# Product-key experts: a tile's output added to x in the eighth head, the differences to the best sum formed by GpSimd

## The chip, the cores and the metric

The kernel runs on one core of a Trainium2 chip. The metric is the device time of one execution in microseconds (us). The core has a matrix engine (TensorE, PE in the profile; its weight loads are PEld), a vector engine (VectorE, DVE), an activation engine (ScalarE, ACT), a general engine (GpSimd, POOL) and SyncE (SP), which only starts transfers here. Each engine works through its own queue in order; they meet at semaphores. SBUF is the on-chip memory of 128 partitions, PSUM the memory that TensorE writes.

## What is computed

The program is a stack of twelve layers on x of 128 x 32 tokens with 128 features, so 4096 rows. The change lies in the third one, a feed-forward layer with product keys. Cut to what matters, for each row of the normalised x:

```
# 8 heads, 2 x 32 keys per head, 1024 experts (i, j), the best 8 are kept
sx = query_x @ keys_x            # 32 similarities per head
sy = query_y @ keys_y            # 32 similarities per head
s[i, j] = sx[i] + sy[j]          # 1024 sums per head
best = the 8 largest s           # among pairs of the 8 best sx and the 8 best sy
share = softmax(best)            # over these 8
value[e] = gelu_tanh(x . down[e])
out = sum over heads and kept experts of share * value[e] * up[e]
x = x + out
```

The kernel does it without gathering: in place of the eight experts it works over all 1024, with exp(s - best) set to zero below the eighth best sum, and divides by the sum of the eight exponentials.

## The kernel before

The 4096 rows are 32 tiles of 128 rows (one per partition). `product_key_experts` first folds the query weights and keys (`query_keys`) and then runs one block in which each engine has a function `phase(t, s, before, after)` for tile t; `s` is the buffer of two, `before` is true where a tile comes ahead of t, `after` where one or two follow. `over_tiles` calls the phases in the same order on all engines, so the work around the change is ordered by hand, by the line at which a step stands in `phase`.

A phase has eight heads, h = 0 to 7, called the first to the eighth head here. Per head:

- GpSimd forms the 1024 sums of two similarities (L751) into one of four buffers, when the product four heads back has freed it. It waits for nothing else but, in the first head, the similarities.
- ScalarE takes the exponential of each half of 512 into a PSUM bank, with minus the best sum as its bias (L790), and scales the identity by the reciprocal of the total into `share` (L795).
- VectorE masks and copies each half: `prob` = (sum >= eighth best) * exponential (L866), the "masking product".
- TensorE multiplies `prob` by `share` in eight blocks (L933, two instructions each) and adds up over the heads in PSUM.

Between the heads stand the steps for the neighbouring tiles. On VectorE, in order: `weigh` of tile t - 1 in the first head (L855, its end lets TensorE start the output, L918, in the fourth head); moments of x of tile t + 2 in the third (L119, L122); bias and MAX8 over the similarities of tile t + 1 in the fourth and fifth (L820, L826); in the sixth the addition of tile t - 1's output to x (L878 to L880, helper L173), which waits for TensorE's `out_done`, and then the cube of the gelu (L846); in the seventh `bests` of tile t + 1 (L829): eight MAX8 over 64 pair sums (L831), a drain, the subtraction `shift` = best eight - best (L833), the negated best as bias (L835). Behind the eighth head come `invert_totals` (L840, L842), which waits for ScalarE's exponential of `shift`, and `gelu` (L850).

GpSimd has, beside the sums, the normalisation factors of tile t + 2 behind the seventh head (L135, L142, L733) and the pair sums of tile t + 1 behind the eighth (L740), for which it waits until the MAX8 of L826 are done. ScalarE has `shift_exp` of tile t + 1 (L771) behind the eighth head, then a normalisation (L766). The first tile's steps are done in a preamble.

Of the kernel before, what the change touches and what calls it, by code (L numbers as in the profile page):

```python
# [16 lines left out]
ALU = mybir.AluOpType  # L17
# [7 lines left out]
P = 128  # L25
# [145 lines left out]
def add_to_x(core, t, update):  # L171

    return core.nc.vector.tensor_tensor(core.x[:, ds(t, 1), :], core.x[:, ds(t, 1), :], update, ALU.add)  # L173
# [488 lines left out]
def product_key_experts(core, name):  # L662
# [8 lines left out]
    nc, dram = core.nc, core.dram  # L671
    H, K, TOP, KG = 8, 32, 8, 16
    E = K * K
    with ExitStack() as outer:
# [14 lines left out]
        pairs = sb("pairs", [P, H, TOP * TOP])  # L689
        best = sb("best", [P, S, H, TOP])  # L690
        shift = sb("shift", [P, H, TOP])
# [17 lines left out]
        half = lambda t, k: t[:, k * HALF:(k + 1) * HALF]  # L709
        shifted_mean = sb("shifted_mean", [P, S])  # L710
        front = Front(core, outer, f"{name}2", S, lambda s: core.psum[:, 7, 0:P])
        (centred, simmed, sims_ready, topped, paired, valued, squared, cubed, tanhed, gelued, cut, exped, inverted, shared, biased, summed, probs, used, kept,
         mixed, out_done) = (core.sem(f"{name}_{n}") for n in (
             "centred", "simmed", "sims_ready", "topped", "paired", "valued", "squared", "cubed", "tanhed", "gelued", "cut", "exped", "inverted", "shared", "biased", "summed", "probs", "used",
             "kept", "mixed", "out_done"))
        block = outer.enter_context(nc.Block())

        def over_tiles(eng, phase):

            phase(0, 0, False, 2)  # L720
            with eng.Fori(0, TILES // 2 - 2) as it:
                phase(1 + 2 * it, 1, True, 2)
                phase(2 + 2 * it, 0, True, 2)
            phase(TILES - 3, 1, True, 2)
            phase(TILES - 2, 0, True, 1)
            phase(TILES - 1, 1, True, 0)

        @block.gpsimd
        def _(pool):
            def normal_factors(t, s):  # L730
                front.pool_rstd(pool, t - s, only=s)
                pool.drain()
                nc.gpsimd.tensor_scalar(shifted_mean[:, s:s + 1], front.mv[:, s, 0:1], front.rstd[:, s, :], -1.0, ALU.mult,  # L733
                                        ALU.mult).then_inc(centred, 1)

            def pair_sums(t, s):
                pool.wait_ge(topped, t + 1)
                sx = top[:, s, 0:H, :].rearrange("p h (i j) -> p h i j", j=1).to_broadcast([P, H, TOP, TOP])
                sy = top[:, s, H:2 * H, :].rearrange("p h (i j) -> p h i j", i=1).to_broadcast([P, H, TOP, TOP])
                nc.gpsimd.tensor_tensor(pairs[:, :, :].rearrange("p h (i j) -> p h i j", j=TOP), sx, sy,  # L740
                                        ALU.add).then_inc(paired, 1)

            def phase(t, s, before, after):
                for h in range(H):
                    if h == 0:
                        pool.wait_ge(sims_ready, t + 1)

                    pool.wait_ge(kept, (t * H + h + 1) * HALVES)
                    sx = sims[:, s, h, :].rearrange("p (i j) -> p i j", j=1).to_broadcast([P, K, K])
                    sy = sims[:, s, H + h, :].rearrange("p (i j) -> p i j", i=1).to_broadcast([P, K, K])  # L750
                    nc.gpsimd.tensor_tensor(sums[:, h % RING, :, :], sx, sy, ALU.add).then_inc(summed, 1)  # L751
                    if after == 2 and h == 6:
                        normal_factors(t + 2, s)
                if after:
                    pair_sums(t + 1, 1 - s)

            normal_factors(0, 0)
            normal_factors(1, 1)
            pair_sums(0, 0)
            over_tiles(pool, phase)  # L760

        @block.scalar
# [53 lines left out]
        @block.vector  # L816
        def _(dve):
            def add_bias(t, s):
                dve.wait_ge(simmed, t + 1)
                nc.vector.tensor_tensor(sims[:, s, :, :].rearrange("p g k -> p (g k)"), SIMS, b_sim[:, :],  # L820
                                        ALU.add).then_inc(sims_ready, 1)
                dve.drain()

            def tops(s, groups):
                for g in groups:
                    ins = nc.vector.max(top[:, s, g, :], sims[:, s, g, :])  # L826
                return ins

            def bests(t, s):  # L829
                for h in range(H):  # L830
                    nc.vector.max(best[:, s, h, :], pairs[:, h, :])  # L831
                dve.drain()
                nc.vector.tensor_tensor(shift[:, :, :], best[:, s, :, :],  # L833
                                        best[:, s, :, 0:1].to_broadcast([P, H, TOP]), ALU.subtract).then_inc(cut, 1)
                nc.vector.tensor_scalar(bias[:, s, :], best[:, s, :, 0:1].rearrange("p h a -> p (h a)"), -1.0, None,  # L835
                                        ALU.mult).then_inc(biased, 1)

            def invert_totals(t, s):
                dve.wait_ge(exped, t + 1)
                nc.vector.tensor_reduce(total[:, s, :], shift[:, :, :], X, ALU.add)  # L840
                dve.drain()
                nc.vector.reciprocal(total[:, s, :], total[:, s, :]).then_inc(inverted, 1)  # L842

            def cube(t, s):
                dve.wait_ge(squared, t + 1)
                nc.vector.scalar_tensor_tensor(cubic[:, :], cubic[:, :], 1.0, pair(2 * s), ALU.add, ALU.mult).then_inc(cubed, 1)  # L846

            def gelu(t, s):
                dve.wait_ge(tanhed, t + 1)
                nc.vector.scalar_tensor_tensor(value[:, s, :], cubic[:, :], 1.0, pair(2 * s), ALU.add,  # L850
                                               ALU.mult).then_inc(gelued, 1)

            def weigh(t, s):
                dve.wait_ge(used, (t + 1) * H + RING)
                nc.vector.scalar_tensor_tensor(weight[:, :], value[:, s, :], 0.5, pair(2 * s), ALU.mult,  # L855
                                               ALU.mult).then_inc(mixed, 1)

            def phase(t, s, before, after):
                o = 1 - s
                for h in range(H):  # L860
                    dve.wait_ge(used, t * H + h + 1)
                    if after and h == 6:
                        dve.wait_ge(paired, t + 2)
                    for k in range(HALVES):
                        dve.wait_ge(probs, (t * H + h) * HALVES + k + 1)
                        nc.vector.scalar_tensor_tensor(  # L866
                            half(prob[:, h % RING, :], k), half(sums[:, h % RING, :, :].rearrange("p i j -> p (i j)"), k),
                            best[:, s, h, TOP - 1:TOP], raw_prob(k), ALU.is_ge, ALU.mult).then_inc(kept, 1)
                    if before and h == 0:
                        weigh(t - 1, o)  # L870
                    if after == 2 and h == 2:
                        front.dve_moments(dve, t + 2 - s, only=s)
                    if after and h == 3:
                        add_bias(t + 1, o)
                        tops(o, range(0, KG // 2))
                    if after and h == 4:
                        tops(o, range(KG // 2, KG)).then_inc(topped, 1)
                    if before and h == 5:  # L878
                        dve.wait_ge(out_done, t)
                        add_to_x(core, t - 1, OUT)  # L880
                    if after and h == 5:
                        cube(t + 1, o)
                    if after and h == 6:
                        bests(t + 1, o)
                if after:
                    invert_totals(t + 1, o)
                    gelu(t + 1, o)

            front.dve_moments(dve, 0, only=0)
            front.dve_moments(dve, 0, only=1)  # L890
            add_bias(0, 0)
            tops(0, range(KG)).then_inc(topped, 1)
            dve.wait_ge(paired, 1)
            cube(0, 0)
            bests(0, 0)
            invert_totals(0, 0)
            gelu(0, 0)
            over_tiles(dve, phase)
            weigh(TILES - 1, 1)
            dve.wait_ge(out_done, TILES)  # L900
            add_to_x(core, TILES - 1, OUT)
# [2437 lines left out]
```

## Time and profile before

| | us |
|---|---|
| median of 3 runs (lowest to highest) | 3903.31 (3892.4 to 3909.63) |
| the profiled execution | 3910.36 |
| its span, first to last instruction | 3908.2 |
| TensorE busy in the span | 3360.9 (86%) |
| VectorE busy | 2672.6 (68%) |
| ScalarE busy | 1648.2 (42%) |
| GpSimd busy | 1231.1 (31%) |

The stage of the change takes some 690 us of the span, from about 389 to 1084 us. The rows of the trace are read like this: a row of a timeline has the start from the span's start, the duration, engine, line, operation, what it writes <- what it reads with the shape, how many instructions the row merges (xN), and in brackets the idle time of the engine just before it and what ended that. Instructions of one engine overlap a little in the records, so the start of the next is a better measure of an instruction's cost than its own duration.

### The profile page before, as it was taken

Reading aid. Unit: us, or ns where it says so; the run is one execution under the profiler, and the core shown is the slowest. Engines: PE = TensorE matmul, PEld = TensorE weight load, DVE = VectorE, ACT = ScalarE, POOL = GpSimd, SP = SyncE. Lnnn points to the kernel's source line nnn. Section 1 sums busy time; section 2 is a strip of 40 time slices with the busy share of each in tenths; the row PEclk is TensorE's granted clock in tenths of the full one; section 3 lists DMA queues with packets and bytes.
Section 4 is the critical chain, followed back from the end, with each engine's and each line's share of the span. In section 5 each row is a group of like instructions: output and inputs, shape, how many; then the busy total and the mean of one; then the engine's idle time right before and its main releaser. Section 6 shows DMA issues by size and latency. Waiting matters only on the chain. (4 is left out here: it accounts for less than half of the span.)

```text
span 3908.2 us, 106170 instructions
## 1 busy us (share of the span) xinstructions
PE 3360.9 (86%) x39854; PEld 2856.4 (73%) x39856; DVE 2672.6 (68%) x7741; ACT 1648.2 (42%) x4070; POOL 1231.1 (31%) x1704
## 2 busy tenths in 40 slices
PE   3787899999968888797899999999999999874756
PEld 2675788888846666545689999999999999743345
DVE  7774899999948888667355555555555555469776
ACT  1231677777727777564122222222222222223342
POOL 3552788888713333303100000000000000145042
PEclk8897999999979999898699999999999999968677
DMA  3000000000012222200275565556555565355000
GB/s 92 4 0 36 1 0 0 0 0 0 1 42 77 76 75 75 58 1 7 45 134 125 121 125 115 125 124 126 125 114 125 125 127 124 64 100 78 1 3 24
DMA packets 374617, 253.41 MB, mean 65 GB/s; under 512 B 118452, under 2 KB 371336, under 8 KB 373672
## 3 DMA queue, kind: packets, MB, share of 16 engines
q1 hardware_dynamic: 369960, 244.92, 28.9%
q10 hardware_dynamic: 4352, 4.20, 0.5%
q8 instruction: 220, 3.60, 0.4%
q14 instruction: 85, 0.70, 0.1%
HBM read 233.01 MB, written 15.75 MB: 64 GB/s over the span
## 5 line engine op out<-in xcount | busy, mean ns | idle before, releaser
L2146 ACT ACTIVATE L_xattn_prob<-psum,L_xattn_nmax 128x258 f32<-128x258 f32 x512 | 239.2, 472 | 958.4 <-DVE L_xattn_nmax L2178 958.4
L933 PE MATMUL psum<-L_ffn_share,L_ffn_prob 128*128 128x128 f32 x4096 | 495.0, 278 | 54.7 <-DVE L_ffn_prob L866 54.7
L2267 PE MATMUL psum<-L_xattn_ctxT,L_xattn_q_ctx 128*128 128x257 f32 x2048 | 523.2, 388 | 9.0 <-issue 4.7
L933 PEld LDWEIGHTS psum<-L_ffn_share,L_ffn_prob 128*128 128x128 f32 x4096 | 472.1, 193 | 73.8 <-DVE L_ffn_prob L866 58.8
L751 POOL TENSOR_TENSOR L_ffn_sums<-L_ffn_sims 128x1024 f32<-128x1024 f32 x256 | 486.6, 1913 | 106.7 <-DVE L_ffn_prob L866 106.7
L2289 PEld LDWEIGHTS psum<-L_xattn_probT,L_xattn_ctx 32*128 32x128 f32 x16384 | 471.1, 187 | 47.0 <-DVE L_xattn_q_ctx L2169 41.0
L2289 PE MATMUL psum<-L_xattn_probT,L_xattn_ctx 32*128 32x128 f32 x16384 | 496.0, 274 | 4.0 <-DVE L_xattn_probT L2192 2.1
L2122 POOL TENSOR_TENSOR L_xattn_z_var<-L_xattn_z_mv,L_xattn_z_eps 128x1 f32<-128x1 f32 x32 | 6.1, 191 | 1328.8 <-DVE L_xattn_z_mv L2204 1295.8
L2267 PEld LDWEIGHTS psum<-L_xattn_ctxT,L_xattn_q_ctx 128*128 128x128 f32 x2048 | 362.0, 191 | 58.0 <-DMA L_xattn_ctx<-ctx_dram 4.8
L790 ACT ACTIVATE psum<-L_ffn_sums,L_ffn_bias 128x512 f32<-128x512 f32 x512 | 340.4, 688 | 94.1 <-DVE L_ffn_prob L866 89.9
L866 DVE SCALAR_TENSOR_TENSOR L_ffn_prob<-L_ffn_sums,L_ffn_best,psum 128x512 f32<-128x512 f32 x512 | 357.8, 740 | 5.7 <-ACT psum L790 2.4
L1223 ACT ACTIVATE L_xattn_prob<-psum,L_xattn_nmax 128x289 f32<-128x289 f32 x512 | 250.0, 501 | 125.0 <-DVE L_xattn_nmax L1250 125.0
L2253 PEld LDWEIGHTS psum<-L_xattn_xnT,L_xattn_m_h 128*128 128x128 f32 x2048 | 269.8, 194 | 20.0 <-issue 4.6
L2253 PE MATMUL psum<-L_xattn_xnT,L_xattn_m_h 128*128 128x128 f32 x2048 | 274.5, 278 | 3.4 <-DVE L_xattn_q_ctx L2169 2.1
L2169 DVE COPY L_xattn_q_ctx<-psum 128x256 f32<-128x256 f32 x512 | 192.5, 415 | 97.5 <-PE psum L2253 97.2
L2278 PEld LDWEIGHTS psum<-L_xattn_u_h,L_xattn_mixed_ctx 128*128 128x128 f32 x2048 | 233.6, 192 | 3.0 <-ACT L_xattn_mixed_ctx L2157 1.3
L2278 PE MATMUL psum<-L_xattn_u_h,L_xattn_mixed_ctx 128*128 128x128 f32 x2048 | 233.9, 275 | 1.1 <-ACT L_xattn_mixed_ctx L2157 1.1
L1250 DVE TENSOR_REDUCE L_xattn_nmax<-psum 128x1 f32<-128x289 f32 x512 | 198.9, 451 | 46.0 <-PE psum L1290 46.0
L2192 DVE STREAM_TRANSPOSE L_xattn_probT<-L_xattn_prob 128x512 f32<-128x512 f32 x256 | 182.1, 711 | 20.1 <-issue 0.9
L2178 DVE TENSOR_REDUCE L_xattn_nmax<-psum 128x2 f32<-128x516 f32 x256 | 178.0, 695 | 20.2 <-issue 1.7
L2186 DVE TENSOR_SCALAR L_xattn_prob<-L_xattn_prob,L_xattn_total 128x256 f32<-128x256 f32 x512 | 161.8, 358 | 20.3 <-issue 0.4
L1290 PE MATMUL psum<-L_xattn_k_all,L_xattn_q_bd 32*128 32x289 f32 x1024 | 100.2, 461 | 79.3 <-POOL L_xattn_k_all L1187 71.8
(439 smaller groups left out, 6149.5 us busy)
## 6 DMA issues: line engine op xcount, KB each, us to landing
L_xattn_ctx<-ctx_dram SPq DMA_DIRECT2D x512, 256.0 KB, 5.4
L_xattn_ctxT<-ctx_T_dram SPq DMA_DIRECT2D x128, 257.0 KB, 3.1
L_xattn_k_all<-ctx_T_dram SPq DMA_DIRECT2D x128, 128.5 KB, 2.1
L_xattn_v_all<-ctx_dram SPq DMA_DIRECT2D x128, 128.0 KB, 2.3
L_attn_qkv_scratch<-L_attn_qkv SPq DMA_DIRECT2D x24, 256.0 KB, 2.8
L_attn_rows<-L_attn_qkv_scratch SPq DMA_DIRECT2D x24, 256.0 KB, 5.2
start_raw<-ctx_dram ACTq DMA_DIRECT2D x16, 256.0 KB, 12.3
start_plug_all<-plug_scratch SPq DMA_DIRECT2D x1, 2048.0 KB, 7.1
```

The lines of the kernel that those rows point to most:

```text
L751: nc.gpsimd.tensor_tensor(sums[:, h % RING, :, :], sx, sy, ALU.add).then_inc(summed, 1)
L790: nc.scalar.activation(raw_prob(k), half(sums[:, h % RING, :, :].rearrange("p i j -> p (i j)"), k), ACT.Exp, bias=bias[:, s, h:h + 1]).the ...
L866: nc.vector.scalar_tensor_tensor(half(prob[:, h % RING, :], k), half(sums[:, h % RING, :, :].rearrange("p i j -> p (i j)"), k), best[:, s, ...
L933: last = nc.tensor.matmul(pair(2 * s)[:, c * P:(c + 1) * P], prob[:, h % RING, c * P:(c + 1) * P], share[:, h % RING, :], start=(h == 0 an ...
L1223: ins = nc.scalar.activation(prob[:, b % 2, g, :], scores(g), ACT.Exp, bias=nmax[:, b % 2, g:g + 1], accum_out=total[:, b % 2, g:g + 1])
L1250: nc.vector.tensor_reduce(nmax[:, b % 2, g:g + 1], scores(g), X, ALU.max, negate=True).then_inc(maxed, 1)
L2146: ins = nc.scalar.activation(prob[:, s, g, :], scores(s)[:, g, :], ACT.Exp, bias=nmax[:, s, g:g + 1], accum_out=total[:, s, g:g + 1])
L2169: nc.vector.tensor_copy(q_ctx[:, p, c, :, 2 * j:2 * j + 2, :], q_bank(k).rearrange("p (h b n) -> p b h n", h=2, b=BT)).then_inc(q_out, 1)
L2253: last = nc.tensor.matmul(q_bank(k)[:, i * P:(i + 1) * P], m_h[:, 2 * j + i, c * P:(c + 1) * P], tokens(t), start=True, stop=True)
L2267: last = nc.tensor.matmul(scores(s)[:, g, 0:CTX], q_ctx[:, p, c, b, h:h + 4, :].rearrange("p h n -> p (h n)"), ctxT[:, b, c, :], start=(c ...
L2278: nc.tensor.matmul(OUT, mixed_ctx[:, r, c * G + i, :], u_h[:, c, 4 * i + r, :], start=(r + c + i == 0), stop=False)
L2289: last = nc.tensor.matmul(mix_bank(r)[:, c * P:(c + 1) * P], ctx[rows, b, k, c * P:(c + 1) * P], probT[rows, b % 2, k, :, :].rearrange("p ...
```

## The change

The addition of tile t - 1's output to x moves in VectorE's phase from the sixth head to the eighth, behind that head's masking product and ahead of `invert_totals`. The subtraction moves from VectorE to GpSimd: VectorE's last MAX8 increments a new semaphore `bested`, GpSimd's new `differences(t, s)` waits for it and increments `cut`, for which ScalarE waits as before. It stands behind the sums of the third head of tile t, and for the first tile in the preamble, behind the first pair sums. The bias stays on VectorE behind the drain.

```diff
--- before.py
+++ after.py
@@ -709,9 +709,9 @@
         half = lambda t, k: t[:, k * HALF:(k + 1) * HALF]
         shifted_mean = sb("shifted_mean", [P, S])
         front = Front(core, outer, f"{name}2", S, lambda s: core.psum[:, 7, 0:P])
-        (centred, simmed, sims_ready, topped, paired, valued, squared, cubed, tanhed, gelued, cut, exped, inverted, shared, biased, summed, probs, used, kept,
+        (centred, simmed, sims_ready, topped, paired, valued, squared, cubed, tanhed, gelued, bested, cut, exped, inverted, shared, biased, summed, probs, used, kept,
          mixed, out_done) = (core.sem(f"{name}_{n}") for n in (
-             "centred", "simmed", "sims_ready", "topped", "paired", "valued", "squared", "cubed", "tanhed", "gelued", "cut", "exped", "inverted", "shared", "biased", "summed", "probs", "used",
+             "centred", "simmed", "sims_ready", "topped", "paired", "valued", "squared", "cubed", "tanhed", "gelued", "bested", "cut", "exped", "inverted", "shared", "biased", "summed", "probs", "used",
              "kept", "mixed", "out_done"))
         block = outer.enter_context(nc.Block())
 
@@ -740,6 +740,11 @@
                 nc.gpsimd.tensor_tensor(pairs[:, :, :].rearrange("p h (i j) -> p h i j", j=TOP), sx, sy,
                                         ALU.add).then_inc(paired, 1)
 
+            def differences(t, s):
+                pool.wait_ge(bested, t + 1)
+                nc.gpsimd.tensor_tensor(shift[:, :, :], best[:, s, :, :], best[:, s, :, 0:1].to_broadcast([P, H, TOP]),
+                                        ALU.subtract).then_inc(cut, 1)
+
             def phase(t, s, before, after):
                 for h in range(H):
                     if h == 0:
@@ -749,6 +754,8 @@
                     sx = sims[:, s, h, :].rearrange("p (i j) -> p i j", j=1).to_broadcast([P, K, K])
                     sy = sims[:, s, H + h, :].rearrange("p (i j) -> p i j", i=1).to_broadcast([P, K, K])
                     nc.gpsimd.tensor_tensor(sums[:, h % RING, :, :], sx, sy, ALU.add).then_inc(summed, 1)
+                    if h == 2 and before:
+                        differences(t, s)
                     if after == 2 and h == 6:
                         normal_factors(t + 2, s)
                 if after:
@@ -757,6 +764,7 @@
             normal_factors(0, 0)
             normal_factors(1, 1)
             pair_sums(0, 0)
+            differences(0, 0)
             over_tiles(pool, phase)
 
         @block.scalar
@@ -828,10 +836,9 @@
 
             def bests(t, s):
                 for h in range(H):
-                    nc.vector.max(best[:, s, h, :], pairs[:, h, :])
-                dve.drain()
-                nc.vector.tensor_tensor(shift[:, :, :], best[:, s, :, :],
-                                        best[:, s, :, 0:1].to_broadcast([P, H, TOP]), ALU.subtract).then_inc(cut, 1)
+                    last = nc.vector.max(best[:, s, h, :], pairs[:, h, :])
+                last.then_inc(bested, 1)
+                dve.drain()
                 nc.vector.tensor_scalar(bias[:, s, :], best[:, s, :, 0:1].rearrange("p h a -> p (h a)"), -1.0, None,
                                         ALU.mult).then_inc(biased, 1)
 
@@ -875,7 +882,7 @@
                         tops(o, range(0, KG // 2))
                     if after and h == 4:
                         tops(o, range(KG // 2, KG)).then_inc(topped, 1)
-                    if before and h == 5:
+                    if before and h == 7:
                         dve.wait_ge(out_done, t)
                         add_to_x(core, t - 1, OUT)
                     if after and h == 5:
```

## Rows read from the trace of the kernel before

**Rows 1.** Busy time by windows: engines with instructions, granted clock, DMA.

```profile
440.00:1060.00 620.00, 576.76 (x4781) 545.08 (x4781) 565.30 (x1491) 462.87 (x848) 502.32 (x348) 1.00 0.00 0
```

**Rows 2.** Groups by line and form, 440 to 1080 us: busy, mean ns | idle before.

```profile
L833 DVE TENSOR_TENSOR L_ffn_shift<-L_ffn_best 128x64 f32<-128x64 f32 x30 | 29.2, 974 | 2.2
...
L173 DVE TENSOR_TENSOR x_sb<-x_sb,psum 128x128 f32 x28 | 8.1, 288 | 32.4 <-PE psum L918 32.4
...
L135 POOL TENSOR_TENSOR L_ffn_front_var_sb<-L_ffn_front_mv_sb,eps 128x1 f32<-128x1 f32 x28 | 5.4, 193 | 0.0
```

**Rows 3.** Timeline of VectorE, from one sixth head to the next.

```profile
714.21 1.39 DVE L866 SCALAR_TENSOR_TENSOR L_ffn_prob<-L_ffn_sums,L_ffn_best,psum 128x512 f32<-128x512 f32 x2
716.76 0.29 DVE L173 TENSOR_TENSOR x_sb<-x_sb,psum 128x128 f32 x1 [1.16 <-PE psum L918]
716.97 1.21 DVE L846 SCALAR_TENSOR_TENSOR L_ffn_cubic<-L_ffn_cubic,psum 128x1024 f32<-128x1024 f32 x1
718.10 1.40 DVE L866 SCALAR_TENSOR_TENSOR L_ffn_prob<-L_ffn_sums,L_ffn_best,psum 128x512 f32<-128x512 f32 x2
719.41 1.10 DVE L831 MAX8 L_ffn_best<-L_ffn_pairs 128x8 f32<-128x64 f32 x8
720.59 0.98 DVE L833 TENSOR_TENSOR L_ffn_shift<-L_ffn_best 128x64 f32<-128x64 f32 x1
721.49 0.16 DVE L835 TENSOR_SCALAR L_ffn_bias<-L_ffn_best 128x8 f32<-128x8 f32 x1
721.56 1.39 DVE L866 SCALAR_TENSOR_TENSOR L_ffn_prob<-L_ffn_sums,L_ffn_best,psum 128x512 f32<-128x512 f32 x2
722.88 0.21 DVE L840 TENSOR_REDUCE L_ffn_total<-L_ffn_shift 128x8 f32<-128x64 f32 x1
...
730.03 0.29 DVE L119 BATCH_NORM_STATS2 L_ffn_front_stats_sb<-x_sb 128x6 f32 x1 [0.21 <-issue]
...
735.44 1.39 DVE L866 SCALAR_TENSOR_TENSOR L_ffn_prob<-L_ffn_sums,L_ffn_best,psum 128x512 f32<-128x512 f32 x2
```

**Rows 4.** Timeline of GpSimd, the same tile.

```profile
714.38 1.07 POOL L740 TENSOR_TENSOR L_ffn_pairs<-L_ffn_top 128x512 f32<-128x512 f32 x1 [0.27 <-DVE L_ffn_top L826]
715.41 3.78 POOL L751 TENSOR_TENSOR L_ffn_sums<-L_ffn_sims 128x1024 f32<-128x1024 f32 x2
719.58 1.91 POOL L751 TENSOR_TENSOR L_ffn_sums<-L_ffn_sims 128x1024 f32<-128x1024 f32 x1 [0.38 <-DVE L_ffn_prob L866]
723.04 1.91 POOL L751 TENSOR_TENSOR L_ffn_sums<-L_ffn_sims 128x1024 f32<-128x1024 f32 x1 [1.55 <-DVE L_ffn_prob L866]
```

**Rows 5.** Timeline of ScalarE, the same tile.

```profile
721.60 0.26 ACT L771 ACTIVATE L_ffn_shift<-L_ffn_shift 128x64 f32<-128x64 f32 x1 [0.81 <-DVE L_ffn_shift L833]
721.77 0.49 ACT L766 ACTIVATE L_ffn_front_xn_sb<-x_sb,L_ffn_shifted_mean,L_ffn_front_rstd_sb 128x128 f32 x1
722.37 1.32 ACT L790 ACTIVATE psum<-L_ffn_sums,L_ffn_bias 128x512 f32<-128x512 f32 x2
```

**Rows 6.** Timelines of VectorE and GpSimd, preamble and the stage's first tile.

```profile
402.67 1.89 DVE L835 TENSOR_SCALAR L_ffn_bias<-L_ffn_best 128x8 f32<-128x8 f32 x1
...
417.99 1.39 DVE L866 SCALAR_TENSOR_TENSOR L_ffn_prob<-L_ffn_sums,L_ffn_best,psum 128x512 f32<-128x512 f32 x2
...
422.93 2.00 DVE L833 TENSOR_TENSOR L_ffn_shift<-L_ffn_best 128x64 f32<-128x64 f32 x1
...
424.92 1.40 DVE L866 SCALAR_TENSOR_TENSOR L_ffn_prob<-L_ffn_sums,L_ffn_best,psum 128x512 f32<-128x512 f32 x2
...
402.62 3.77 POOL L751 TENSOR_TENSOR L_ffn_sums<-L_ffn_sims 128x1024 f32<-128x1024 f32 x2
...
419.19 5.65 POOL L751 TENSOR_TENSOR L_ffn_sums<-L_ffn_sims 128x1024 f32<-128x1024 f32 x3
```

**Rows 7.** Timeline of TensorE: the output of the tile ahead.

```profile
714.66 1.95 PE L918 MATMUL psum<-L_ffn_up,L_ffn_weight 128*128 128x128 f32 x16
```

## Prediction

> **What bounds the kernel now.** I read the profile from the outside in. The diff touches one stage, the product-key experts, so the first view is the table by windows for the even part of that stage [rows 1]: in 620 us TensorE is busy for 576.76 us (93%), VectorE for 565.30 us (91%), GpSimd for 502.32 us (81%) and ScalarE for 462.87 us (75%), at a granted clock of 1.00. Two engines are nearly full, so the next question is which of them the other waits for. The timeline of VectorE answers it [rows 3]: its instructions follow each other at once, and the one idle time of more than 0.25 us in a tile is the 1.16 us before the addition to x (L173). The groups by line [rows 2] say the same of the sum: 32.4 us of idle time in front of 28 of these additions, 1.16 us each. So VectorE sets the pace with two blemishes: it waits for TensorE's output at L173, and its subtraction L833, 64 elements wide, takes 0.974 us on average [rows 2].
>
> I take as zero of a tile the start of the sixth head's masking product (L866, h = 5): 714.21 in one tile, 735.44 in the next [rows 3]. The period is 21.23 us. Counted from that zero, before: the addition to x at +2.55, the cube L846 at +2.76, the seventh head's product at +3.89, the eight MAX8 at +5.20, the subtraction at +6.38, the bias (L835) at +7.28, the eighth head's product at +7.35 and the sum of the exponentials (L840) at +8.67. Everything from there to the next zero is 21.23 - 8.67 = 12.56 us of VectorE work which the diff leaves alone. So the question is by how much +8.67 moves.
>
> **Why the subtraction is slow.** At +6.38 it starts, and it ends at 721.57. GpSimd's pair sums of the third head (L751) run from 719.58 to 721.49 [rows 4]. In the stage's first tile it starts at 422.93 and ends at 424.93; GpSimd's three sums from 419.19 end at 424.84 [rows 6]. Twice it ends 0.08 to 0.09 us behind GpSimd's instruction, whatever its own length. It is not the subtraction alone: the bias instruction L835, 8 elements, takes 0.16 us in most tiles and 1.89 us at 402.67, where GpSimd had begun a sum at 402.62 that lasts about 1.9 us [rows 6]. Both wait until GpSimd's instruction lets go. This is what the page SBUF — State Buffer of the Trainium skill (section "SBUF: two separate sides") states as an exclusive lock on a shared pair of ports, for VectorE instructions with two SBUF inputs or in a two-port mode; the trace agrees for both kinds (0.98 and 1.89 us). The rule speaks against this change, since the bias, with one input and its output in SBUF, stays on VectorE; a sum that leaves the lock out would be the 2.14 us a tile worked out next.
>
> **Part 1: the addition moves from the sixth head to the eighth.** At its old place it costs the wait and itself: the product at 714.21 is followed at 716.76, and the cube at 716.97. In the first tile, which has no addition there, the same steps run freely [rows 6]: zero at 417.99, the instruction behind the MAX8s at 422.93, which is +4.94 against +6.38. So 1.44 us go. TensorE's output ended at 716.61 [rows 7], +2.40, so at its new place (+8.2) the result has long been there; the wait is free. The addition itself still costs 716.97 - 716.76 = 0.21 us. Its address is computed by a register instruction; the idle "issue" time before L119, which has one too, is 0.21 us [rows 3], so this is between 0 and 0.21 us more. I take 0.03, as there is no drain in front of the addition behind which it would have to stand. Nobody waits for x soon: its moments were taken long before, and the next output of TensorE follows three heads later.
>
> **Part 2: the subtraction leaves VectorE.** Its start to the bias's start was 0.90 us. Taken at face value, both parts give 1.44 + 0.90 - 0.21 = 2.13 to 2.14 us a tile, 64 us over 30 tiles. That is not what I expect. The bias now comes straight behind the MAX8s, at +4.94. GpSimd, counted from the same zero: pair sums at +0.17 (714.38), head 1 at +1.20 (715.41), head 2 at +1.20 + 3.78 - 1.91 = +3.07, and so head 3 at +4.94, unless VectorE holds it up; before it started only at 719.58, +5.37, since it waited for the seventh head's product [rows 4]. With that product 1.44 us earlier, that wait is gone and head 3 starts at +4.94, the very time of the bias. Exactly this is seen in the first tile: GpSimd at 419.19 + 5.65 - 1.91 = 422.93, VectorE at 422.93, and VectorE lost: 2.00 us [rows 6]. There the eighth head's product starts at 424.92; with the bias as the waiting instruction and nothing behind it, at about 424.85, +6.86. Before it was +7.35. So parts 1 and 2 together bring that product forward by 0.49 us, and the addition behind it takes 0.21 to 0.24 back: 0.25 us a tile.
>
> **Part 3: GpSimd's differences.** The trace shows no 64-element instruction on GpSimd. The nearest rows are 0.19 us for one element [rows 2] and 1.07 us for 512 [rows 4]; with 1.91 us for 1024 the slope is 1.64 ns per element and 64 elements come to 0.34 us. I take 0.34, between 0.19 and 1.07. They stand behind head 3's sums, which end at +6.85; done at +7.2. ScalarE's exponential (0.26 us, begun 0.03 us behind the subtraction's end [rows 5]) then ends at +7.5. VectorE needs it at 6.86 + 1.32 + 0.24 = +8.4. It is covered by 0.9 us; were the cover gone, each further us would be a us. On GpSimd the differences have head 4's sums behind them, which wait for the eighth head's product and start at 723.04 after an idle time of 1.5 us [rows 4]; so they cost it nothing. On ScalarE the exponential has a normalisation and the next tile's first exponentials behind it (721.77 and 722.37 [rows 5]), which VectorE wants only 2 us later. The new semaphore costs an increment on the last MAX8, which is nothing here.
>
> **Part 4: the ends.** In the preamble GpSimd now waits for the first tile's MAX8s, until about 402.2, before it sums head 1, where it had finished two sums. VectorE's first bias in turn no longer stands 1.89 us behind GpSimd [rows 6]. I put these at plus or minus 1 us together, once. The last tile ends on TensorE and gains nothing.
>
> **The sum.** 30 tiles have both the addition and the MAX8s. 30 x 0.25 = 7.5 us of the profiled execution's 3910.36 us: 3902.9. The median of the runs shown, 3903.31, is 0.18% below that execution, so in its terms 3903.3 - 7.5 = 3895.8, about 3896. With the register instruction at 0 to 0.21 us and 1 us for the preamble, this case reaches from 3893 to 3903.
>
> **The rivals.** (a) *The bias gets in first.* VectorE and GpSimd arrive within 0.01 us of each other, and whichever is a few hundredths of a us early keeps the other out. If it is the bias, it takes 0.16 us, head 3's sums run from +5.10 to +7.0, the differences end at +7.35, the exponential at +7.64, and L840 starts at +7.67 in place of +8.67; the addition disappears in that wait. That is 1.0 us a tile, 30 us, 3873; so the 2.14 us are out of reach even then, and TensorE, 93% busy, would be close at 19.7 us of 20.2. For it speaks that the tie is so near; against it, that VectorE lost the one tie and the one arrival 0.05 us late that the trace has. A mixture of tiles lies in between; it passes 0.5% when about half to two thirds of the tiles go this way. (b) *The lock goes from GpSimd to GpSimd.* The differences are queued directly behind head 3's sums; if they are served before the bias, it waits 0.34 us longer, the product starts at +7.20, and 0.15 - 0.24 = -0.09 us a tile: 3 us slower, 3906. Against it: at 402.6 VectorE was let in between two sums. (c) *Slower: the differences are slow on GpSimd.* Their broadcast restarts every eight elements, and the trace has no such width. L840 then waits at +6.85 + c + 0.3. From c = 1.2 us the gain shrinks, from 1.52 us it is a loss, and 0.5% is lost from 2.2 us on; at c = 2.5 us it is 1.0 us a tile, 30 us, 3933. Against it: twice the 1.07 us of an instruction with eight times the elements.
>
> **How the numbers follow.** Forecast 0.60, (a) 0.22, (b) 0.12, (c) 0.06. The predicted time is the forecast's, 3896. The range takes in (a) and (b) and leaves (c) out: 3871 to 3909. A measurement here tells 0.5% from no change, 19.5 us. Faster by more than that is (a), 0.22; within it are the forecast and (b), 0.72; slower is (c), 0.06.
>
> **What would show it.** In the changed kernel's trace: no idle time before L173's new place, and none before the cube; the bias instruction at about 1.9 to 2.0 us in nearly every tile, ending 0.08 us behind GpSimd's third sum; GpSimd's third sum directly behind its second; the differences at 0.3 to 0.4 us and no wait of L840 for ScalarE; a period of 20.98 us. A bias of 0.16 us in most tiles with a wait before L840 is (a); one of 2.3 us is (b); a long wait before L840 with long differences is (c). A period under 20 us would say that my account of the two engines' exclusion is wrong.

## The result, and the profile after

Over twenty runs each the changed kernel takes 3881.33 us (median; 3872.95 to 3894.76) and the kernel before 3900.55 us (3892.4 to 3909.63). The ratio is 0.9954 with a 95% interval of 0.9944 to 0.9964: 18 us, 0.46%, faster, with an interval of 14 to 22 us (the medians themselves lie 19.2 us apart). I forecast 7.5 us, and a range of 3871 to 3909 us. The sign and the class (less than 0.5%) came out; the size is more than twice mine. About 5.5 us of that lie in the stage of the change and are explained below; the rest lies outside it.

First where the time lies. The moments of x (L119) mark the stage: their first start here and their first start in the next layer. Columns: how many, shortest/median/longest in ns, first and last start. Before:

```profile
L119 DVE BATCH_NORM_STATS2 L_ffn_front_stats_sb<-x_sb x32: 293/294/296, 389.1 to 1026.5; 128x6 f32 x28, 128x6 f32<-128x128 f32 x4
L119 DVE BATCH_NORM_STATS2 L_xattn_front_stats_sb<-x_sb x32: 274/276/295, 1086.2 to 1133.5; 128x6 f32 x32
```

After:

```profile
L119 DVE BATCH_NORM_STATS2 L_ffn_front_stats_sb<-x_sb x32: 293/294/296, 383.0 to 1008.2; 128x6 f32 x28, 128x6 f32<-128x128 f32 x4
L119 DVE BATCH_NORM_STATS2 L_xattn_front_stats_sb<-x_sb x32: 274/278/295, 1067.1 to 1114.0; 128x6 f32 x32
```

1086.2 - 389.1 = 697.1 us became 1067.1 - 383.0 = 684.1 us: 13.0 us less in the stage (12.9 before rounding). The spans, 3908.2 and 3881.3 us, differ by 26.9 us: 6.1 us of that are there already when the stage begins, and 7.8 us come behind it, and at neither place was an instruction altered. A difference of two single executions is not a measurement of this change; the stage by itself is.

Now the tile. VectorE after, from the start of the sixth head's product (my zero) to the next; L873 is the masking product that was L866, L842 the bias that was L835, L847 the sum that was L840:

```profile
702.20 1.39 DVE L873 SCALAR_TENSOR_TENSOR L_ffn_prob<-L_ffn_sums,L_ffn_best,psum 128x512 f32<-128x512 f32 x2
703.50 1.22 DVE L853 SCALAR_TENSOR_TENSOR L_ffn_cubic<-L_ffn_cubic,psum 128x1024 f32<-128x1024 f32 x1
704.63 1.40 DVE L873 SCALAR_TENSOR_TENSOR L_ffn_prob<-L_ffn_sums,L_ffn_best,psum 128x512 f32<-128x512 f32 x2
705.95 1.11 DVE L839 MAX8 L_ffn_best<-L_ffn_pairs 128x8 f32<-128x64 f32 x8
707.15 1.92 DVE L842 TENSOR_SCALAR L_ffn_bias<-L_ffn_best 128x8 f32<-128x8 f32 x1
708.99 1.39 DVE L873 SCALAR_TENSOR_TENSOR L_ffn_prob<-L_ffn_sums,L_ffn_best,psum 128x512 f32<-128x512 f32 x2
710.31 0.27 DVE L173 TENSOR_TENSOR x_sb<-x_sb,psum 128x128 f32 x1
710.50 0.20 DVE L847 TENSOR_REDUCE L_ffn_total<-L_ffn_shift 128x8 f32<-128x64 f32 x1
...
722.96 1.39 DVE L873 SCALAR_TENSOR_TENSOR L_ffn_prob<-L_ffn_sums,L_ffn_best,psum 128x512 f32<-128x512 f32 x2
```

GpSimd beside it:

```profile
702.37 1.07 POOL L740 TENSOR_TENSOR L_ffn_pairs<-L_ffn_top 128x512 f32<-128x512 f32 x1 [0.27 <-DVE L_ffn_top L834]
703.39 5.65 POOL L756 TENSOR_TENSOR L_ffn_sums<-L_ffn_sims 128x1024 f32<-128x1024 f32 x3
709.00 0.29 POOL L745 TENSOR_TENSOR L_ffn_shift<-L_ffn_best 128x64 f32<-128x64 f32 x1
710.46 1.91 POOL L756 TENSOR_TENSOR L_ffn_sums<-L_ffn_sims 128x1024 f32<-128x1024 f32 x1 [1.17 <-DVE L_ffn_prob L873]
```

Against [rows 3] the wait in front of the cube is gone and so is the subtraction, but the bias, an instruction over eight elements, has grown from 0.16 to 1.92 us. It starts at +4.95 and ends at 709.07 (707.15 + 1.92). GpSimd's three sums no longer pause before the third, as they did in [rows 4]; the third starts at 703.39 + 5.65 - 1.91 = 707.13, 0.02 us ahead of the bias, and ends at 709.04. The eighth head's product comes at +6.79 in place of +7.35, and the addition takes part of that back. The period shown is 20.76 us in place of 21.23 us. Over all 32 tiles the bias has these durations (shortest/median/longest), so it is so nearly everywhere:

```profile
L842 DVE TENSOR_SCALAR L_ffn_bias<-L_ffn_best x32: 300/1920/1928, 396.1 to 1039.0; 128x8 f32<-128x8 f32 x32
```

### The profile page after: what moved, and what is told of

It is laid out like the page before. It is cut to its first block and busy times, and to the rows that moved or that the text cites. A ratio compares the mean times of both kernels' runs of the same rounds, so it can differ in the third digit from the quotient of the medians.

```text
span 3881.3 us, 106172 instructions
## 1 busy us (share of the span) xinstructions
PE 3347.8 (86%) x39856; PEld 2848.1 (73%) x39856; DVE 2692.2 (69%) x7709; ACT 1645.6 (42%) x4070; POOL 1237.4 (32%) x1736
## 5 line engine op out<-in xcount | busy, mean ns | idle before, releaser
L873 DVE SCALAR_TENSOR_TENSOR L_ffn_prob<-L_ffn_sums,L_ffn_best,psum 128x512 f32<-128x512 f32 x512 | 357.7, 739 | 7.9 <-ACT psum L798 3.6
## 6 DMA issues: line engine op xcount, KB each, us to landing
start_raw<-ctx_dram ACTq DMA_DIRECT2D x16, 256.0 KB, 12.2
```

Of the source, the lines that this page charges most:

```text
L873: nc.vector.scalar_tensor_tensor(half(prob[:, h % RING, :], k), half(sums[:, h % RING, :, :].rearrange("p i j -> p (i j)"), k), best[:, s, ...
```

## The experiments

Seven kernels, with 4 to 12 runs each, beside 20 runs of the kernel before for the first four and 9 for the last three. The table has the difference of the medians to the kernel before in the same comparison (before: 3896.66 us beside the first four, 3896.99 us beside the last three), the stage's length in the run's own profile less the 697.1 us of before, and the start of the eighth head's product from my zero. The last column is what is left of the span outside the stage.

| kernel | median us | to before | ratio (95%) | stage, to before | eighth head at | rest |
|---|---|---|---|---|---|---|
| before (profile above) | | | | 697.1 | +7.35 | 3211 |
| after (profile above) | | | | -13.0 | +6.79 | 3197 |
| after_again | 3881.95 | -14.7 | 0.9957 (0.9940 to 0.9973) | -12.8 | | 3201 |
| e1_add_only | 3891.32 | -5.3 | 0.9983 (0.9972 to 0.9993) | -7.4 | +6.92 | 3197 |
| e2_diff_only | 3886.39 | -10.3 | 0.9973 (0.9962 to 0.9984) | -4.8 | +7.22 | 3195 |
| e3_bias_reduce | 3855.00 | -41.7 | 0.9894 (0.9879 to 0.9910) | -39.1 | +5.17 | 3189 |
| e6_split | 3864.18 | -32.8 | 0.9917 (0.9904 to 0.9931) | -34.5 | +5.93 | 3196 |
| e4_diff_first | 3836.50 | -60.5 | 0.9841 (0.9827 to 0.9854) | -60.2 | +5.17 | 3203 |
| e5_both | 3834.55 | -62.4 | 0.9838 (0.9824 to 0.9852) | -60.0 | | 3195 |

### Is the rest of the program part of it?

> The changed kernel unaltered, to separate the stage from the rest. The stage of product-key experts, from its first moments of x to the next layer's, took 697.1 us in the profile before and 684.2 us in the profile after, 12.9 us less, while the medians differ by 19 us. Theory one: the other 6 us are scatter of the rest of the program between executions; then this run's rest (span less the stage) differs from 3197.1 us (that of the profile after) by several us while its stage is again 684 us, and its time lies 13 to 19 us under before. Theory two: the change alters something outside the stage; then the rest is again 3197 us and the time again 19 us under.

The stage is again 12.8 us shorter, from 390.2 to 1074.5 us, while the rest is 3201 us and not 3197 us. Over all nine profiles the rest runs from 3189 to 3211 us, and the profile before is its upper end. In the other six kernels the differences of medians lie from 5.5 us beyond the stage's (e2) to 2.1 us short of it (e1), on both sides. The kernel before itself had a median of 3900.55 us in the first comparison and 3896.66 us in this one, with nothing altered. And the scatter goes with the clock that TensorE was granted on average: of the twenty runs of after, the nine at 0.920 to 0.922 took 3879.47 to 3894.76 us, the seven at 0.925 to 0.928 took 3872.95 to 3881.23 us. The even part of the stage, 440 to 940 us, ran at 1.00 before and after, so that part of the scatter lies elsewhere. So theory one is the better supported: about 13 us come from the stage, and the 1.9 to 6.2 us more in the medians are of the size by which the rest scatters. That is no proof that none of it belongs to the change; the median of twenty runs is 19 us, and what would make the remaining 6 us was not found in any stage.

### Each part alone

> Before with the addition to x in the eighth head alone; the subtraction stays on VectorE. Theory of the exclusion: with the 1.16 us wait gone VectorE reaches the subtraction at +4.94 us from the sixth head's product, when GpSimd begins its third sum; the subtraction lasts 2.0 us in every tile in place of 0.98, the eighth head's product starts at +6.9 in place of +7.35, and the addition gives back 0.14 to 0.19. So 0.26 to 0.31 us a tile, 8 to 9 us in all. Rival: the two parts add up independently, and this one frees 1.44 - 0.19 = 1.25 us a tile, 37 us.

```diff
@@ -877,3 +877,3 @@
                         tops(o, range(KG // 2, KG)).then_inc(topped, 1)
-                    if before and h == 5:
+                    if before and h == 7:
                         dve.wait_ge(out_done, t)
```

VectorE's subtraction in that kernel, all 32 tiles (shortest/median/longest):

```profile
L833 DVE TENSOR_TENSOR L_ffn_shift<-L_ffn_best x32: 887/1992/1997, 398.1 to 1046.9; 128x64 f32<-128x64 f32 x32
```

And a tile on VectorE's timeline:

```profile
707.09 1.38 DVE L866 SCALAR_TENSOR_TENSOR L_ffn_prob<-L_ffn_sums,L_ffn_best,psum 128x512 f32<-128x512 f32 x2
...
712.02 1.99 DVE L833 TENSOR_TENSOR L_ffn_shift<-L_ffn_best 128x64 f32<-128x64 f32 x1
713.93 0.16 DVE L835 TENSOR_SCALAR L_ffn_bias<-L_ffn_best 128x8 f32<-128x8 f32 x1
714.01 1.39 DVE L866 SCALAR_TENSOR_TENSOR L_ffn_prob<-L_ffn_sums,L_ffn_best,psum 128x512 f32<-128x512 f32 x2
```

GpSimd's timeline of the same tile:

```profile
708.27 5.65 POOL L751 TENSOR_TENSOR L_ffn_sums<-L_ffn_sims 128x1024 f32<-128x1024 f32 x3
```

The subtraction doubled, from 0.976 us in the median to 1.99 us, because it now starts when GpSimd's third sum does (708.27 + 5.65 - 1.91 = 712.01, against 712.02). Most of the 1.16 us of waiting that were removed came back there. Of the 37 us of the rival 7.4 are there in the stage and 5.3 in the medians, against the 8 to 9 us expected.

> After with the addition to x back in the sixth head; the differences stay on GpSimd. Theory of the exclusion: the bias starts at +6.4 where the subtraction did and lasts until GpSimd's third sum ends, at +7.3, so some 0.9 us in place of 0.16; the eighth head's product starts at +7.2 to +7.3 in place of +7.35: 0.05 to 0.12 us a tile, 2 to 4 us in all. Rival: the 0.90 us of the subtraction are saved, 27 us.

```diff
@@ -884,3 +884,3 @@
                         tops(o, range(KG // 2, KG)).then_inc(topped, 1)
-                    if before and h == 7:
+                    if before and h == 5:
                         dve.wait_ge(out_done, t)
```

The bias in that kernel, all 32 tiles:

```profile
L842 DVE TENSOR_SCALAR L_ffn_bias<-L_ffn_best x32: 299/902/1152, 395.0 to 1047.3; 128x8 f32<-128x8 f32 x32
```

The bias inherits the wait of the subtraction that stood there: 0.90 us in place of 0.16. The stage is 4.8 us shorter, a little more than the 2 to 4 us that I expected; the rival asked for 27 us. The medians show 10.3 us, with an interval of 6 to 15 us from the ratio; 5.5 us of it are not in the stage. The two parts alone give 7.4 + 4.8 = 12.2 us of the stage, both together 13.0: they do add up, but to a fifth of the 64 us, since each is cut short by the same thing.

### Is it the kind of instruction?

> After with the bias formed by a negated maximum over one element (a reduction) in place of a multiplication by -1; same engine, place, input and output. In the trace before, reductions and reciprocals of this size ran 0.20 us beside GpSimd's sums. Theory: the form of the instruction decides whether it must wait for GpSimd; the bias then takes 0.1 to 0.3 us, the eighth head's product starts at +5.0 to +5.2, and the sum of the exponentials becomes the next wait: differences end at +7.1, the exponential at +7.4, the reduction at +7.45 in place of +8.30. That is 0.85 us a tile, 25 us less than after. Rival: any VectorE instruction behind the MAX8s and the drain is held at this place; then it takes 1.9 us again and the time is that of after.

```diff
@@ -841,4 +841,3 @@
                 dve.drain()
-                nc.vector.tensor_scalar(bias[:, s, :], best[:, s, :, 0:1].rearrange("p h a -> p (h a)"), -1.0, None,
-                                        ALU.mult).then_inc(biased, 1)
+                nc.vector.tensor_reduce(bias[:, s, :], best[:, s, :, 0:1], X, ALU.max, negate=True).then_inc(biased, 1)
 
```

A tile on VectorE's timeline in that kernel:

```profile
709.83 1.39 DVE L872 SCALAR_TENSOR_TENSOR L_ffn_prob<-L_ffn_sums,L_ffn_best,psum 128x512 f32<-128x512 f32 x2
...
714.79 0.17 DVE L842 TENSOR_REDUCE L_ffn_bias<-L_ffn_best 128x8 f32<-128x8 f32 x1
715.00 1.41 DVE L872 SCALAR_TENSOR_TENSOR L_ffn_prob<-L_ffn_sums,L_ffn_best,psum 128x512 f32<-128x512 f32 x2
716.32 0.28 DVE L173 TENSOR_TENSOR x_sb<-x_sb,psum 128x128 f32 x1
717.25 0.22 DVE L846 TENSOR_REDUCE L_ffn_total<-L_ffn_shift 128x8 f32<-128x64 f32 x1 [0.65 <-ACT L_ffn_shift L779]
```

GpSimd's timeline of the same tile:

```profile
711.03 5.65 POOL L756 TENSOR_TENSOR L_ffn_sums<-L_ffn_sims 128x1024 f32<-128x1024 f32 x3
```

This decides it. The same engine, place, input and output, 0.17 us in place of 1.92, while GpSimd's third sum runs from 714.77 (716.68 - 1.91) to 716.68 (711.03 + 5.65). The eighth head's product moves to +5.17. Then the next wait appears where the expectation had it: the sum of the exponentials stands 0.65 us for ScalarE and starts at +7.42 (7.45 expected). The stage gives 26 us beyond after, against 25 expected.

The Trainium skill's page SBUF — State Buffer (section "SBUF: two separate sides") names the two kinds that wait, instructions with two SBUF inputs and those in a two-port mode. The trace agrees that the subtraction waits, and the multiplication too; in which mode the multiplication runs, no row shows. That the reduction is free to go is shown by these runs.

### Is it as long as GpSimd's instruction?

> After with GpSimd's sums of the third head in two instructions of 512 elements in place of one of 1024; the other heads are unaltered. Theory of the exclusion: the bias waits for one GpSimd instruction, so it lasts about 1.0 us in place of 1.92, ending behind the first half; the eighth head's product starts at +5.9; the sum of the exponentials then waits for the differences at +7.2 and the exponential, to about +7.5 in place of +8.30: 0.8 us a tile, 20 to 25 us less than after. Rival one: the wait has a length of its own and stays 1.9 us. Rival two: GpSimd's two halves are served back to back and the bias waits for both; then nothing is gained.

```diff
@@ -755,3 +755,8 @@
                     sy = sims[:, s, H + h, :].rearrange("p (i j) -> p i j", i=1).to_broadcast([P, K, K])
-                    nc.gpsimd.tensor_tensor(sums[:, h % RING, :, :], sx, sy, ALU.add).then_inc(summed, 1)
+                    if h == 2:
+                        nc.gpsimd.tensor_tensor(sums[:, h % RING, 0:K // 2, :], sx[:, 0:K // 2, :], sy[:, 0:K // 2, :], ALU.add)
+                        nc.gpsimd.tensor_tensor(sums[:, h % RING, K // 2:K, :], sx[:, K // 2:K, :], sy[:, K // 2:K, :],
+                                                ALU.add).then_inc(summed, 1)
+                    else:
+                        nc.gpsimd.tensor_tensor(sums[:, h % RING, :, :], sx, sy, ALU.add).then_inc(summed, 1)
                     if h == 2 and before:
```

A tile on VectorE's timeline in that kernel:

```profile
714.52 1.39 DVE L878 SCALAR_TENSOR_TENSOR L_ffn_prob<-L_ffn_sums,L_ffn_best,psum 128x512 f32<-128x512 f32 x2
...
719.48 1.06 DVE L847 TENSOR_SCALAR L_ffn_bias<-L_ffn_best 128x8 f32<-128x8 f32 x1
720.45 1.39 DVE L878 SCALAR_TENSOR_TENSOR L_ffn_prob<-L_ffn_sums,L_ffn_best,psum 128x512 f32<-128x512 f32 x2
```

GpSimd's timeline of the same tile:

```profile
719.45 1.06 POOL L757 TENSOR_TENSOR L_ffn_sums<-L_ffn_sims 128x512 f32<-128x512 f32 x1
720.46 1.05 POOL L758 TENSOR_TENSOR L_ffn_sums<-L_ffn_sims 128x512 f32<-128x512 f32 x1
721.47 0.30 POOL L745 TENSOR_TENSOR L_ffn_shift<-L_ffn_best 128x64 f32<-128x64 f32 x1
```

The bias ends at 720.54, 0.03 us behind the end of the first half (719.45 + 1.06), and the second half has begun at 720.46 all the same. So the wait lasts one GpSimd instruction, and VectorE is served between two that stand back to back: rivals one and two both fall. The stage gives 21.5 us beyond after, within the 20 to 25 expected, although GpSimd does the same sums with one instruction more.

### The order on GpSimd

> After with GpSimd's differences ahead of the third head's sums in place of behind them; nothing else. Theory of the exclusion: the MAX8s end at +4.9, GpSimd comes out of its second sum at +4.94 and forms the differences (0.29 us); the bias waits only for these, to +5.3, or slips in ahead; the eighth head's product starts at +5.2 in place of +6.79, the exponential is ready at +5.6. That frees 1.6 us a tile, of which TensorE, at some 19.2 to 19.7 us of work a tile, lets 1.1 to 1.5 us through: 33 to 45 us less than after. Rival: the bias is held by something else than GpSimd's 1.9 us sums; then it takes 1.9 us again and nothing is gained.

```diff
@@ -751,2 +751,4 @@
                         pool.wait_ge(sims_ready, t + 1)
+                    if h == 2 and before:
+                        differences(t, s)
 
@@ -756,4 +758,2 @@
                     nc.gpsimd.tensor_tensor(sums[:, h % RING, :, :], sx, sy, ALU.add).then_inc(summed, 1)
-                    if h == 2 and before:
-                        differences(t, s)
                     if after == 2 and h == 6:
```

A tile on VectorE's timeline in that kernel:

```profile
704.34 1.39 DVE L873 SCALAR_TENSOR_TENSOR L_ffn_prob<-L_ffn_sums,L_ffn_best,psum 128x512 f32<-128x512 f32 x2
...
709.29 0.30 DVE L842 TENSOR_SCALAR L_ffn_bias<-L_ffn_best 128x8 f32<-128x8 f32 x1
709.51 1.39 DVE L873 SCALAR_TENSOR_TENSOR L_ffn_prob<-L_ffn_sums,L_ffn_best,psum 128x512 f32<-128x512 f32 x2
...
712.51 1.40 DVE L873 SCALAR_TENSOR_TENSOR L_ffn_prob<-L_ffn_sums,L_ffn_best,psum 128x512 f32<-128x512 f32 x2
713.91 1.22 DVE L862 SCALAR_TENSOR_TENSOR L_ffn_weight<-L_ffn_value,psum 128x1024 f32<-128x1024 f32 x1
```

GpSimd's timeline of the same tile:

```profile
709.28 0.29 POOL L745 TENSOR_TENSOR L_ffn_shift<-L_ffn_best 128x64 f32<-128x64 f32 x1
709.53 3.78 POOL L758 TENSOR_TENSOR L_ffn_sums<-L_ffn_sims 128x1024 f32<-128x1024 f32 x2
```

The bias now meets the differences, 0.29 us, in place of a sum of 1.91 us, and lasts 0.30 us. The stage is 60.2 us shorter than before, 47 us shorter than after, just over the 33 to 45 us expected. What stands in the way next is in the table by windows, 440 to 940 us; the first busy time after the length is TensorE's:

```profile
440.00:940.00 500.00, 498.02 (x4238) 479.40 (x4237) 483.39 (x1300) 411.63 (x754) 450.58 (x338) 1.00 0.00 0
```

TensorE is busy for 498.0 of 500 us, at the granted clock of 1.00; in [rows 1] it was 93%. And VectorE now waits for it once a tile: `weigh` (L862), which needs all of the last tile's products on TensorE, starts 1.40 us behind the masking product ahead of it (712.51 to 713.91), where it is 1.31 us in after; over the tiles the step behind the product's second half is 0.74 us in place of 0.66. Of the 1.61 us by which the eighth head's product came forward, 1.52 us reached the period (20.76 to 19.24 us), and the rest went into this wait. TensorE is full, or within half a per cent of it; VectorE, busy for 483.4 of the 500 us, is not far behind, and how much more could be got on VectorE alone was not tested.

> Differences ahead of the third head's sums and the bias as a negated maximum over one element. If the exclusion is the only cause, the bias no longer waits for the 0.29 us differences either: 0.2 us a tile more than with the differences first alone, up to 6 us in all where VectorE still sets the pace, 0 where TensorE does.

It has the edits of e3 and e4 together. The bias is down to 0.17 us, the stage is 60.0 us shorter, as with e4 alone, and the medians, 3834.55 and 3836.50 us with overlapping ratio intervals, can't be told apart. TensorE is busy for 498.03 of the same 500 us, and the step to `weigh` is 0.74 us again. But this is no test of what VectorE's time is worth there, since hardly any was saved: the bias's own duration fell from 0.30 to 0.17 us, yet the eighth head's product came at +5.16 in place of +5.17 in the median, as it starts 0.21 us behind the start of the reduction and 0.22 us behind that of the briefly held multiplication. The 0.2 us a tile of the expectation came from durations; what counts is the start of the next instruction. Either of these two beats both kernels of the study: 1.6% faster than before, and some 45 us faster than the change as it was made. The only edit that it takes is to form the differences one instruction earlier in GpSimd's queue.

## Why the prediction was right, and where its sizes were off

**What bounds the stage, and the wait in front of the addition:** right. VectorE set the pace; the cube now follows the sixth head's product at 703.50 - 702.20 = 1.30 us, the wait is gone, and none stands at the addition's new place.

**The wait that takes its place:** right, and shown. The main step of the prediction was that a plain sum of the parts (2.14 us a tile, 64 us) would not come, since the bias would arrive when GpSimd begins its third sum and would last 1.9 to 2.0 us. It lasts 1.92 us in the median. e3 (other form of instruction), e6 (half the length) and e4 (another instruction of GpSimd in its way) each move exactly this wait.

**Who wins the near tie:** rival (a), that the bias goes first, got 0.22. In all 30 tiles that count, the bias lasted 1.92 us, within 0.01 us; GpSimd was ahead every time, by 0.01 to 0.03 us. In e1 the two starts lie within 0.01 us of each other in the records, on either side, and the subtraction lasted 1.99 us, within 0.01 us, in all 30 tiles too. I had read it off the stage's first tile [rows 6], and that one row was a good guide.

**Rivals (b) and (c):** fell. The bias ended 0.03 us behind the third sum and did not wait for the differences; these took 0.29 us on GpSimd where I had 0.34. I had called the 2.14 us a tile of the plain sum out of reach even under (a). That was too strong: e4 has 60 of those 64 us. The estimate of 19.7 us of TensorE's work a tile, with which I argued it, was too high as well, as e4's whole period is 19.24 us.

**The sizes.** I forecast 0.25 us a tile and 7.5 us. The additions to x lie 614.1 us apart over 29 periods before (441.3 to 1055.4) and 601.8 us after (440.4 to 1042.2): 21.18 and 20.75 us, so 0.42 us a tile. Two terms of the sum were mis-sized. The start of the eighth head's product was put at +6.86 and came at +6.79, as I let the bias end 0.09 us behind GpSimd like the subtraction; it ended 0.03 us behind: 0.07 us a tile, 2 us.

And what the addition gives back was put at 0.24 us. It costs 0.19 us in its new place (710.31 to 710.50), but the whole gave back only 0.56 - 0.42 = 0.14 us. The other 0.05 us are the reciprocal behind it: before, 14 of the reciprocals stand behind 2.7 us of idle time without a releaser, one in each of the 14 passes of the loop over tiles, and after none does. Every reciprocal has 0.07 us of idle time ahead of it in both kernels, so the excess is 2.7 - 14 x 0.07 = 1.7 us, or 0.06 us for each of the 30 tiles. That idle time goes with the subtraction's place and not with the addition's: e1, with the subtraction on VectorE, has the same 2.7 us in 14 tiles, and e2, with the differences on GpSimd, has none. Why the subtraction's place brings it about, the runs do not tell.

The two terms make some 5 us. From the sixth head's product of the second tile to that of the last, 30 periods, it is 633.25 us before (438.70 to 1071.95) and 620.59 us after (432.26 to 1052.85): 12.7 us of the stage's 13.0. The other 0.3 us lie ahead of that, in the preamble and the first tile, where I had put plus or minus 1.

**Outside the stage:** nothing was predicted there, and up to 6 us of the measured 19 are there. The forecast's own reach ended at 3893, and its 13 us in the stage would have given 3890 against the 3903 that I started from; the kernel before turned out at 3900.55 over twenty runs, and the stage's 13 us put after at 3887.5 on that footing. The measured 3881.33 lies inside the range only because that took in rival (a), which did not happen. That is a range that held for the wrong reason.

## What to carry to other kernels

When a wait on VectorE is removed, look at what GpSimd is doing at the time at which the next VectorE instruction now arrives: in this kernel a subtraction with two SBUF inputs, and a multiplication by a constant from SBUF to SBUF, stood until GpSimd's current instruction ended, with 64 and with 8 elements. The profile books that as the instruction's own duration and not as idle time, so a small instruction with a long duration is the sign to look for. Before shaving such instructions, see whether they can be of a form that doesn't wait (a reduction here, though it costs 0.21 us to the next instruction's start, where the multiplication that nothing holds costs 0.07), or let GpSimd have something short in its queue at that place; an instruction moved by one position was worth 47 us more, where the whole change was worth 13. And judge a small change by the stage it lies in: the two single spans here differed by 14 us outside the stage.

## What the runs showed of the hardware that I had not expected

The held instruction leaves at once: a multiplication over 8 elements ended 0.03 us behind GpSimd's instruction, the subtraction over 64 elements with two inputs 0.08 to 0.09 us behind, and GpSimd's next instruction started on time in both cases: in e6 at 720.46 behind 719.45, where 512 elements take 1.05 us, and in the preamble of before at 402.62 [rows 6], where the sum ahead of it ended at 402.66 and the subtraction that it had held at 402.75. A reduction over the same 8 elements took 0.166 to 0.168 us in all 32 tiles of e3, each time beside a running GpSimd instruction. On GpSimd 64 elements took 0.29 us, 512 took 1.05 to 1.07 us and 1024 took 1.91 us.
